# Two groups' expert choice in five pieces, their places and scatters three steps later

## The chip, the cores and the metric

The kernel runs on one core of a Trainium2 chip, as one launch. The metric is the device time of that launch in microseconds (us), lower is better. The core's engines work in parallel, each through its own instruction queue in order: TensorE (PE, with its weight loads PEld), VectorE (DVE), ScalarE (ACT), GpSimd (POOL), and the DMA queues, of which SyncE (SP) and ScalarE issue plain transfers and GpSimd the indirect ones. They synchronise by semaphores.

## The reference

Two layers over x of shape 32 x 128 x 128 (batch row, token, feature), float32. Layer 0 is cross attention with 16 heads of width 8 and a mixture of 8 experts; layer 1 is cross attention with 16 heads of width 64 and a quantised feed-forward net. The change touches the routing of layer 0:

```python
x = x + xattn0(layernorm(x), ctx, ctx)
# routing, on inputs = layernorm(x):
num = einsum('bsd,ed->bse', inputs, waff)
aff = num / (norm(inputs) * norm(waff) + 1e-09)
tcr = one_hot(argmax(softmax(aff)), 8)            # each token's one expert
ecr = (rank of the token in its row by aff) < cap
out = sum over experts e of gelu(xi @ W1[e] + b1[e]) @ W2[e] + b2[e],  xi = inputs * (tcr * ecr)[e]
x = x + out
```

The kernel sorts the tokens by expert before the expert stage: each token gets a place (a row of the buffer sorted_x), and an indirect DMA scatters a batch row's 128 tokens there.

## The kernel before

**Stages.** Layer 0's attention with the routing woven in (0 to about 245 us of the span), the experts (to about 348 us), layer 1 (to the end). The change lies in the first stage.

**Steps.** The first stage is a loop over 32 batch rows, b = 0 to 31, written once for each engine; the same b on all engines is called a step. TensorE's step b: scores(b) (L366), minus_max(b, 0) (L373), route_transpose(b-4) (L307), places(q) in some steps (L341 to L346), back_transposes(b-1) (L392), minus_max(b, 1), affinity(b-4) (L325), max_scores(b+1, 0) (L357), o_transpose(b-1) (L397), x_transpose(b+2), minus_max(b, 2 and 3), output(b-1) (L401), projections(b+2) (L312 to L314), max_scores(b+1, 1), values(b) (L385).

VectorE's step b: locate(q) in some steps, normalise(b-1) (L595, L598; it waits for the back transposes), num_copy(b-4) (L542), x_stats(b+4), two maxima (L589), residual(b-1) (L604), choose(q) in some steps, q_spread(b+2) (L531; it waits for the projections), v_copy(b+2) (L537), two maxima, residual_stats(b-1) (L608, L610).

GpSimd's step b: x_plus(b) (L196, read by residual(b)), route_norm(b-2) (L221 to L225; it waits for residual_stats(b-2) and makes xn2, which route_transpose reads), x_norm(b+4) (L185 to L190; up to step 27), denominators(q) in some steps (L234 to L244), then scatters (L251). ScalarE makes the exponentials and copies, among them route_copy (L465), which takes the routing transpose out of PSUM into r_xnT.

**Groups.** Routing works on groups of batch rows: (0, 8), (8, 16), (16, 24), (24, 28), (28, 32), q = 0 to 4. For a group ending at row z the denominators are made in step z+1, choose(q) in step z+3 (ten small VectorE instructions, L550 to L569, each waiting for the one before by the semaphore choice), places(q) on TensorE and locate(q) on VectorE (four instructions, L576 to L583) in step z+4. That is steps 11 and 12 for group 0, 19 and 20 for group 1, 27 and 28 for group 2; groups 3 and 4 lie at the loop's end and behind it.

**Waits.** route_transpose(r) waits until v_copy(r+5) is done, since it writes the PSUM bank that the projections were read from. places(q) waits for tcrb of its group and for the route_copy of the routing transpose just ahead of it. The affinity after it waits for the first instruction of locate(q), which reads the places from the same bank. A scatter waits for all four of locate(q). At the loop's start ScalarE's DMA queue clears sorted_x, in steps 1 to 12.

**Scatters.** From step 13 on, GpSimd issues one scatter a step where a located row is left (group 0: steps 13 to 20, group 1: steps 21 to 28), and up to three a step from step 29; the rest follow behind the loop. Only when all 32 have landed does the expert stage load its first tile.

Of the kernel before, what the change touches and what calls it, by code (L numbers as in the profile page):

```python
# [5 lines left out]
ALU = mybir.AluOpType  # L6
# [65 lines left out]
def attention_routing_block(nc, ctx, space, consts, x, ctxT, w, wr, x_res, xn2, stats2, psum, dram):  # L72
# [7 lines left out]
    E = 8  # L80
    GROUPS = ((0, 8), (8, 16), (16, 24), (24, 28), (28, 32))
    NG = len(GROUPS)
    group_at = {z - 1: q for q, (a, z) in enumerate(GROUPS)}
    group_of = {r: q for q, (a, z) in enumerate(GROUPS) for r in range(a, z)}
    SCALE = float(HD) ** -0.5
    LOADS = ((0, 1), (1, 2), (2, 4), (4, 8), (8, 16), (16, 32))
# [91 lines left out]
    def pool_part(g, after_setup, before_last):  # L178
# [84 lines left out]
        for b in range(B):  # L263
            if b == 1:
                expert_norms()
            x_plus(b, b % 2)
            if b >= 2:
                route_norm(b - 2)
            if b + 4 < B:
                x_norm(b + 4, b % 2)  # L270
            if b - 2 in group_at:
                denominators(group_at[b - 2])
            located = max([z for a, z in GROUPS if z + 5 <= b], default=0)
            for _ in range(1 if b < 29 else 3):
                if b >= 13 and scattered < located:
                    scatter(scattered)
                    scattered += 1
        route_norm(B - 2)
# [9 lines left out]
    def tensor_part(pe):  # L288
# [31 lines left out]

        def affinity(r):
            pe.wait_ge(rsem["xnT"], r + 1)
            if r - 1 in group_at:
                pe.wait_ge(rsem["place"], 4 * group_at[r - 1] + 1)
            nc.tensor.matmul(nump, rt["xnT"][:, r % 2, :], rt["waffT"][:], start=True, stop=True).then_inc(rsem["num_done"], 1)  # L325

        def places(q):
            a, z = GROUPS[q]
            n = z - a
            at_, rows = placep[:, 0:n * E], rt["tcrb"]  # L330
            pe.wait_ge(rsem["choice"], 10 * q + 7)
            pe.wait_ge(rsem["set"], 7)
            if z + 5 <= B:
                pe.wait_ge(rsem["xnT"], z + 1)
            else:
                pe.wait_ge(rsem["num"], z)
            wait(pe, rsem["choice"], 10 * (q - 1) + 10)
            if q == NG - 1:
                pe.wait_ge(rsem["choice"], 10 * q + 10)
                nc.tensor.matmul(countp, rt["ones_b"][:], rt["seen"][:, q + 1, :], start=True, stop=True)  # L340
            nc.tensor.matmul(at_, rt["before_t"][:], rows[:, a:z, :].rearrange("p b e -> p (b e)"),  # L341
                             start=True, stop=False, skip_group_check=True)
            for j in range(n - 1):
                nc.tensor.matmul(placep[:, E * (j + 1):E * n], rt["ones_b"][:], rows[:, a + j:a + j + 1, :].broadcast_to([P, n - 1 - j, E]),
                                 start=False, stop=False, skip_group_check=True)
            nc.tensor.matmul(at_, rt["ones_b"][:], rt["seen"][:, q:q + 1, :].broadcast_to([P, n, E]),  # L346
                             start=False, stop=True, skip_group_check=True).then_inc(rsem["place_done"], 1)
# [60 lines left out]
        for b in range(B):  # L408
            s, more = b % 2, b + 2 < B
            scores(b)  # L410
            minus_max(b, 0)
            if b >= 4:
                route_transpose(b - 4)
            if b - 5 in group_at:
                places(group_at[b - 5])
            if b == 0:
                expert_sums()
            else:
                back_transposes(b - 1, 1 - s)
            minus_max(b, 1)  # L420
            if b >= 4:
                affinity(b - 4)
            if b + 1 < B:
                max_scores(b + 1, 0)
            if b >= 1:
                o_transpose(b - 1, 1 - s)
            if more:
                x_transpose(b + 2, s)
            minus_max(b, 2)
            minus_max(b, 3)  # L430
            if b >= 1:
                output(b - 1, 1 - s)
            if more:
                projections(b + 2, s)
            if b + 1 < B:
                max_scores(b + 1, 1)
            values(b)
# [77 lines left out]
    def vector_part(dve):  # L515
# [25 lines left out]
            dve.wait_ge(rsem["num_done"], r + 1)  # L541
            nc.vector.tensor_copy(rt["num"][:, r, :], nump).then_inc(rsem["num"], 1)  # L542

        def choose(q):
            a, z = GROUPS[q]
            cols, n, seq, first = slice(a, z), z - a, rsem["choice"], 10 * q
            aff, tcr, shape = rt["aff"][:, cols, :], rt["tcr"][:, cols, :], [P, z - a, E]
            tmp, score, smax = rt["tmp"][:, 0:n, :], rt["score"][:, 0:n, :], rt["smax"][:, 0:n]
            dve.wait_ge(rsem["den"], 5 * q + 5)
            nc.vector.reciprocal(tmp, rt["den"][:, q % 2, 0:n, :]).then_inc(seq, 1)  # L550
            dve.wait_ge(seq, first + 1)
            dve.wait_ge(rsem["num"], z)
            nc.vector.tensor_tensor(aff, rt["num"][:, cols, :], tmp, ALU.mult).then_inc(seq, 1)
            dve.wait_ge(seq, first + 2)
            nc.vector.tensor_reduce(rt["mval"][:, cols], aff, AX_X, ALU.max).then_inc(seq, 1)
            dve.wait_ge(seq, first + 3)
            nc.vector.tensor_tensor(tmp, aff, rt["mval"][:, cols].unsqueeze(2).broadcast_to(shape), ALU.is_equal).then_inc(seq, 1)
            dve.wait_ge(seq, first + 4)
            dve.wait_ge(rsem["set"], 6)
            nc.vector.tensor_tensor(score, tmp, rt["weight"][:].unsqueeze(1).broadcast_to(shape), ALU.mult).then_inc(seq, 1)  # L560
            dve.wait_ge(seq, first + 5)
            nc.vector.tensor_reduce(smax, score, AX_X, ALU.max).then_inc(seq, 1)
            dve.wait_ge(seq, first + 6)
            nc.vector.tensor_tensor(rt["tcrb"][:, cols, :], score, smax.unsqueeze(2).broadcast_to(shape), ALU.is_equal).then_inc(seq, 1)
            nc.vector.tensor_tensor(tcr, score, smax.unsqueeze(2).broadcast_to(shape), ALU.is_equal).then_inc(seq, 1)
            dve.wait_ge(seq, first + 8)
            nc.vector.tensor_reduce(rt["gsum"][:], tcr.rearrange("p b e -> p e b"), AX_X, ALU.add).then_inc(seq, 1)
            dve.wait_ge(seq, first + 9)
            nc.vector.tensor_tensor(rt["seen"][:, q + 1, :], rt["seen"][:, q, :], rt["gsum"][:], ALU.add).then_inc(seq, 1)  # L569

        def locate(q):
            a, z = GROUPS[q]
            cols, n, seq, first = slice(a, z), z - a, rsem["place"], 4 * q
            place = rt["place"][:, 0:n, :]
            dve.wait_ge(rsem["place_done"], q + 1)
            nc.vector.tensor_tensor(place, placep[:, 0:n * E].rearrange("p (b e) -> p b e", e=E),  # L576
                                    rt["region"][:].unsqueeze(1).broadcast_to([P, n, E]), ALU.add).then_inc(seq, 1)
            dve.wait_ge(seq, first + 1)
            nc.vector.tensor_tensor(place, place, rt["tcr"][:, cols, :], ALU.mult).then_inc(seq, 1)
            dve.wait_ge(seq, first + 2)  # L580
            nc.vector.tensor_reduce(rt["posf"][:, cols], place, AX_X, ALU.add).then_inc(seq, 1)
            dve.wait_ge(seq, first + 3)
            nc.vector.tensor_copy(rt["pos_s"][:, cols], rt["posf"][:, cols]).then_inc(seq, 1)  # L583

        def maxima(b, s, k):
            dve.wait_ge(max_done, 4 * b + k + 1)
# [33 lines left out]
            maxima(0, 0, k)  # L620
        for b in range(B):
            s, more = b % 2, b + 2 < B
            if b - 5 in group_at:
                locate(group_at[b - 5])
            if b == 0:
                dve.wait_ge(rsem["wsum_done"], 1)
                nc.vector.tensor_copy(rt["wsum"][:], yp[:, 0:E]).then_inc(rsem["wsum"], 1)
            else:
                normalise(b - 1, 1 - s)
            if b >= 4:  # L630
                num_copy(b - 4)
            if b + 4 < B:
                x_stats(b + 4, s)
            if b + 1 < B:
                maxima(b + 1, 1 - s, 0)
                maxima(b + 1, 1 - s, 1)
            if b >= 1:
                residual(b - 1, 1 - s)
            if b - 4 in group_at:
                choose(group_at[b - 4])  # L640
            if more:
                q_spread(b + 2, s)
                v_copy(b + 2, s)
            if b + 1 < B:
                maxima(b + 1, 1 - s, 2)
                maxima(b + 1, 1 - s, 3)
            if b >= 1:
                residual_stats(b - 1, 1 - s)
# [1579 lines left out]
```

## Time and profile before

| | |
|---|---|
| median of 3 runs | 924.01 us (922.65 to 928.94) |
| profiled execution | 923.75 us |
| its span, first to last instruction | 922.0 us |
| mean granted TensorE clock | 0.970 of full |
| busy share of the span: PE, DVE, ACT, POOL | 92%, 74%, 47%, 52% |

The page gives the span in 40 slices of 23 us with each engine's busy share; the first stage fills the first eleven. A timeline row gives start, duration, engine, line, operation, output and inputs, the count merged into the row, and in brackets the idle time ahead of it with what ended that.

### The profile page before, as it was taken

The page shows a single profiled execution, that of the slowest core. Times are in us where ns is not written, and L with a number is a line of the kernel's source. Part 1 is how long each engine was busy: PE and PEld are TensorE (multiplying, and loading weights), DVE is VectorE, ACT ScalarE, POOL GpSimd, SP SyncE. Part 2 cuts the span into 40 slices and gives each one's busy share as a digit, 9 for nine tenths or more (in the row PEclk, how much of TensorE's full clock was granted, in tenths as well). Part 3 has the DMA queues.
Part 4 walks back from the last instruction along what each step waited for, and adds up shares of the span by engine and source line. Part 5 has one row for each costly group of instructions (what it writes and reads, how often), then busy time and mean ns, then how long its engine had stood idle before and what let it go on. Part 6 is the DMA issues. An engine that isn't in the chain of part 4 may idle for free.

```text
span 922.0 us, 28047 instructions
## 1 busy us (share of the span) xinstructions
PE 849.0 (92%) x9989; PEld 682.0 (74%) x10019; DVE 683.1 (74%) x1915; ACT 432.4 (47%) x1010; POOL 482.7 (52%) x977
## 2 busy tenths in 40 slices
PE   2999999997599997999999999999999999999964
PEld 1677777765598885787877878878878788787752
DVE  2688888886524565588888888888888888888866
ACT  1566565654156563335354454444544545444432
POOL 5567687877522224245554654545646555454331
PEclk9999999999799997999999999999999999999995
DMA  7666430001556650121121121211212112112120
GB/s 206 224 247 242 157 102 15 14 14 33 154 141 169 160 154 26 34 57 33 33 63 37 45 54 34 62 37 34 62 36 54 45 34 62 37 34 57 28 56 9
DMA packets 57980, 71.33 MB, mean 77 GB/s; under 512 B 8051, under 2 KB 34547, under 8 KB 57843
## 3 DMA queue, kind: packets, MB, share of 16 engines
q1 hardware_dynamic: 43842, 45.48, 19.2%
q10 hardware_dynamic: 11952, 19.86, 5.8%
q0 software_dynamic: 2048, 4.20, 1.5%
q8 instruction: 82, 1.34, 0.6%
q14 instruction: 56, 0.45, 0.2%
HBM read 45.13 MB, written 24.38 MB: 75 GB/s over the span
## 4 chain that ended last, share of the span: by engine, by line
PE 81%; DVE 7%; POOL 5%; issue 4%; DMA 1%; ACT 1%; SPq 1%; DVEq 0%; POOLq 0%; ACTq 0%
PE psum L1596 8%; PE psum L1526 7%; PE psum L1613 7%; PE psum L1517 7%; PE psum L1575 6%; PE psum L1555 6%; PE psum L868 4%; PE psum L1601 4%; PE psum L1624 3%; PE psum L858 3%; PE psum L366 3%; PE psum L373 2%; PE psum L1586 2%; PE psum L385 2%; PE psum L357 1%
## 5 line engine op out<-in xcount | busy, mean ns | idle before, releaser
L1768 ACT ACTIVATE a_pT<-psum 128x512 f32<-128x512 f32 x128 | 69.5, 595 | 53.9 <-PE psum L1601 53.9
L1360 POOL TENSOR_TENSOR f_hd<-f_hmc,f_wmean 128x1 f32<-128x1 f32 x32 | 6.8, 211 | 151.6 <-DVE f_hr L2020 151.6
L1526 PEld LDWEIGHTS psum<-a_cTm,a_Wk 128*128 128x128 f32 x512 | 62.9, 194 | 28.6 <-issue 27.2
L589 DVE TENSOR_REDUCE l_mx<-psum 128x4 bf16<-128x512 f32 x128 | 81.5, 678 | 1.8 <-PE psum L357 1.4
L1907 DVE TENSOR_REDUCE a_mxf<-psum 128x4 f32<-128x512 f32 x128 | 80.9, 672 | 1.3 <-PE psum L1586 1.3
L1596 PE MATMUL psum<-a_qT,a_kT 64*128 64x128 f32 x1024 | 74.4, 285 | 5.2 <-ACT a_v L1790 1.1
L1517 PEld LDWEIGHTS psum<-a_xT,a_Wq 128*128 128x128 f32 x512 | 66.1, 196 | 15.3 <-issue 14.4
L475 ACT ACTIVATE l_pT<-psum 128x512 f32<-128x512 f32 x128 | 70.5, 597 | 11.7 <-PE psum L373 11.5
L1526 PE MATMUL psum<-a_cTm,a_Wk 128*128 128x128 f32 x512 | 74.0, 289 | 1.9 <-POOL a_cTm L1317 1.1
L1596 PEld LDWEIGHTS psum<-a_qT,a_kT 64*128 64x128 f32 x1024 | 62.1, 187 | 14.5 <-issue 14.0
L1517 PE MATMUL psum<-a_xT,a_Wq 128*128 128x128 f32 x512 | 71.1, 283 | 0.5 <-ACT a_xT L1751 0.5
L1575 PE MATMUL psum<-a_Wv,a_cTm 128*128 128x512 f32 x128 | 69.9, 628 | 1.2 <-DVE a_kT L1895 0.7
L1613 PE MATMUL psum<-a_pT,a_v 128*64 128x128 f32 x1024 | 70.0, 279 | 0.0
L1895 DVE TENSOR_TENSOR a_kT<-psum,a_nkm 128x512 f32<-128x512 f32 x64 | 42.5, 664 | 36.5 <-PE psum L1526 36.5
L1555 PE MATMUL psum<-a_Wo,a_oT 128*128 128x128 f32 x512 | 64.3, 280 | 5.5 <-DVE a_oT L1930 5.5
L1555 PEld LDWEIGHTS psum<-a_Wo,a_oT 128*128 128x128 f32 x512 | 61.4, 196 | 6.1 <-DVE a_oT L1930 6.0
L1808 ACT COPY f_hqT<-psum 128x512 bf16<-128x512 bf16 x32 | 18.7, 585 | 99.9 <-PE psum L1661 99.9
L827 POOL COPY e_w2t<-e_w 128x512 f32 x39 | 24.3, 625 | 74.5 <-PE psum L868 74.5
L1613 PEld LDWEIGHTS psum<-a_pT,a_v 128*64 128x64 f32 x1024 | 54.6, 136 | 11.2 <-issue 7.0
L1354 POOL TENSOR_SCALAR f_hq<-f_ht 128x512 bf16<-128x512 f32 x29 | 56.5, 1948 | 2.3
L373 PEld LDWEIGHTS psum<-negI,l_mx 128*128 128x128 bf16 x512 | 36.4, 103 | 25.9 <-DVE l_mx L589 22.7
L1790 ACT COPY a_v<-psum 128x512 f32<-128x512 f32 x64 | 37.5, 585 | 25.4 <-PE psum L1575 25.4
(298 smaller groups left out, 2180.9 us busy)
## 6 DMA issues: line engine op xcount, KB each, us to landing
sorted_x<-r_zeros ACTq DMA_DIRECT2D x12, 1408.0 KB, 5.9
a_r_all<-a_r_rows SPq DMA_DIRECT2D x64, 256.0 KB, 4.0
e_w<-in_E_W1b SPq DMA_DIRECT2D x39, 258.0 KB, 2.8
e_xt<-sorted_x SPq DMA_DIRECT2D x39, 64.0 KB, 2.4
sorted_y<-e_yt ACTq DMA_DIRECT2D x39, 64.0 KB, 2.4
a_cin<-in_ctx SPq DMA_DIRECT2D x32, 64.0 KB, 3.7
out<-f_x SPq DMA_DIRECT2D x32, 64.0 KB, 3.2
x_res<-in_x SPq DMA_DIRECT2D x1, 512.0 KB, 5.9
```

Source lines behind the costliest of these rows:

```text
L373: last = nc.tensor.matmul(tp[k][:, j * S:(j + 1) * S], mx[:, b % 2, h:h + 1].to_broadcast([P, P]), negI[:], start=False, stop=(j == Q4 - 1 ...
L475: nc.scalar.activation(pT[:, k, :], tp[k], ACT.Exp, scale=SCALE).then_inc(exp_ready, 1)
L589: nc.vector.tensor_reduce(mx[:, s, Q4 * k:Q4 * k + Q4], maxp[k % 2].rearrange("p (h t) -> p h t", h=Q4), AX_X, ALU.max).then_inc(mx_ready, 1)
L1354: nc.gpsimd.tensor_scalar(hq[:], ht[:], -M, 127.0, ALU.add, ALU.min).then_inc(hq_ready, 1)
L1517: last = nc.tensor.matmul(bank[:, i * S:(i + 1) * S], Wq[:, 4 * half + i, :], xT[:, b % 2, :], start=True, stop=True)
L1526: last = nc.tensor.matmul(bank[:, i * S:(i + 1) * S], Wk[:, 4 * half + i, :], cTm[:, b % 2, :], start=True, stop=True)
L1555: nc.tensor.matmul(pa[:, 0:D], oT[:, p, :], Wo[:, p, :], start=(p == 0), stop=False)
L1575: nc.tensor.matmul(bank, cTm[:, b % 2, :], Wv[:, 512 * half:512 * half + 512], start=True, stop=True).then_inc(v_done, 1)
L1596: nc.tensor.matmul(tp[e][:, i * S:(i + 1) * S], kT[r, b % 2, p, :], qT[r, b % 2, p, :], start=(i == 0), stop=False, skip_group_check=True)
L1613: last = nc.tensor.matmul(op[half][e * HD:(e + 1) * HD, i * S:(i + 1) * S], v[:, b % 2, 8 * half + 4 * e + i, :], pT[:, 2 * half + e, i * ...
L1768: nc.scalar.activation(pT[:, 2 * half + e, :], tp[e], ACT.Exp, scale=SCALE).then_inc(exp_ready, 1)
L1907: nc.vector.tensor_reduce(mxf[:, hh:hh + 4], maxp[e].rearrange("p (h t) -> p h t", h=Q4), AX_X, ALU.max).then_inc(mxf_ready, 1)
```

## The change

choose(q) is cut into five functions. For groups 0 and 1 (SPREAD = 2) one of them runs in each of the steps z+2 to z+6 (10 to 14, 18 to 22), at the place in the step where choose stood. places(q) and the first half of locate(q) move from step z+4 to z+7 (15 and 23), and locate's second half to the place of the choice pieces in the same step. The affinity's wait moves with them; places(q) waits for the route_copy of its new step. Scatters start the step after: group 0 in steps 16 to 23, one a step; group 1 in steps 24 to 27, two a step. Groups 2 to 4 stay as they were. No instruction's operands change.

```diff
+    SPREAD = 2
+    close_at = {z + (7 if q < SPREAD else 4): q for q, (a, z) in enumerate(GROUPS)}
...
-            located = max([z for a, z in GROUPS if z + 5 <= b], default=0)
-            for _ in range(1 if b < 29 else 3):
-                if b >= 13 and scattered < located:
+            located = max([GROUPS[q][1] for c, q in close_at.items() if c < b], default=0)
+            for _ in range(1 if b < 24 else 2 if b < 29 else 3):
+                if scattered < located:
                     scatter(scattered)
...
         def affinity(r):
             pe.wait_ge(rsem["xnT"], r + 1)
-            if r - 1 in group_at:
-                pe.wait_ge(rsem["place"], 4 * group_at[r - 1] + 1)
+            if r + 4 in close_at:
+                pe.wait_ge(rsem["place"], 4 * close_at[r + 4] + 1)
...
         def places(q):
-            if z + 5 <= B:
+            if q < SPREAD:
+                pe.wait_ge(rsem["xnT"], z + 4)
+            elif z + 5 <= B:
                 pe.wait_ge(rsem["xnT"], z + 1)
...
-            if b - 5 in group_at:
-                places(group_at[b - 5])
+            if b in close_at:
+                places(close_at[b])
...
+        def choose_spread(q, part):      # 0 reciprocal, 1 affinity, 2 score, 3 expert, 4 seen
...
-            if b - 5 in group_at:
-                locate(group_at[b - 5])
+            if b in close_at:
+                locate_rows(close_at[b])
+                if close_at[b] >= SPREAD:
+                    locate_position(close_at[b])
...
-            if b - 4 in group_at:
+            if b - 4 in group_at and group_at[b - 4] >= SPREAD:
                 choose(group_at[b - 4])
+            for q in range(SPREAD):
+                choose_spread(q, b - GROUPS[q][1] - 2)
+            if b in close_at and close_at[b] < SPREAD:
+                locate_position(close_at[b])
```

## Rows read from the trace of the kernel before

**Rows 1.** Windows: bounds, length, each engine's busy us (instructions), PEclk, DMA share, GB/s.
```profile
96.11:104.53 8.42, 6.63 (x103) 4.84 (x99) 7.50 (x26) 3.81 (x9) 3.63 (x7) 1.00 0.44 172
104.53:110.41 5.88, 5.88 (x94) 4.49 (x90) 4.91 (x15) 3.70 (x9) 3.44 (x7) 1.00 0.64 245
145.68:155.42 9.74, 7.96 (x102) 6.13 (x99) 7.49 (x26) 3.88 (x9) 8.09 (x14) 0.82 0.05 15
196.57:206.51 9.94, 7.99 (x102) 6.13 (x98) 7.22 (x24) 3.88 (x9) 6.46 (x11) 0.83 0.05 16
```

**Rows 2.** Timeline of VectorE, step 10, the query spread of an ordinary step.
```profile
89.36 0.75 DVE L531 SCALAR_TENSOR_TENSOR l_qz<-psum,l_bq,group_rows 128x512 f32<-128x512 f32 x1 [0.58 <-PE psum L314]
```

**Rows 3.** Timeline of VectorE, step 11, group 0's choice and the query spread behind it.
```profile
94.57 0.54 DVE L550 RECIPROCAL r_tmp<-r_den 128x64 f32<-128x64 f32 x1
95.15 0.22 DVE L553 TENSOR_TENSOR r_aff<-r_num,r_tmp 128x64 f32<-128x64 f32 x1
...
95.66 0.41 DVE L557 TENSOR_TENSOR r_tmp<-r_aff,r_mval 128x64 f32<-128x64 f32 x1
...
96.36 0.22 DVE L562 TENSOR_REDUCE r_smax<-r_score 128x8 f32<-128x64 f32 x1
...
96.76 0.22 DVE L565 TENSOR_TENSOR r_tcr<-r_score,r_smax 128x64 f32<-128x64 f32 x1
...
97.42 0.75 DVE L531 SCALAR_TENSOR_TENSOR l_qz<-psum,l_bq,group_rows 128x512 f32<-128x512 f32 x1
```

**Rows 4.** Timeline of TensorE, step 12, and one row of step 20 (150.82).
```profile
97.19 0.40 PE L373 MATMUL psum<-negI,l_mx 128*128 128x128 bf16 x4
98.51 0.30 PE L307 MATMUL psum<-ident,xy 128*128 128x128 f32 x1 [0.93 <-DVE l_v L537]
99.26 0.19 PE L341 MATMUL psum<-r_tcrb,r_before_t 128*128 128x64 bf16 x1 [0.45 <-ACT r_xnT L465]
...
99.49 0.63 PE L392 MATMUL psum<-ident,l_oev 128*128 128x128 f32 x4
...
101.34 0.33 PE L397 MATMUL psum<-ident,l_on 128*128 128x128 f32 x1 [0.41 <-DVE l_on L598]
...
150.82 0.47 PE L397 MATMUL psum<-ident,l_on 128*128 128x128 f32 x1 [0.37 <-DVE l_on L598]
```

**Rows 5.** Timeline of TensorE, step 18, an ordinary one.
```profile
134.99 0.40 PE L373 MATMUL psum<-negI,l_mx 128*128 128x128 bf16 x4
135.23 0.28 PE L307 MATMUL psum<-ident,xy 128*128 128x128 f32 x1
135.34 0.60 PE L392 MATMUL psum<-ident,l_oev 128*128 128x128 f32 x4
...
136.62 0.33 PE L397 MATMUL psum<-ident,l_on 128*128 128x128 f32 x1
```

**Rows 6.** Timeline of GpSimd, steps 17 to 19, and VectorE's residual of step 19.
```profile
129.90 0.23 POOL L221 TENSOR_SCALAR r_vpe<-stats 128x1 f32<-128x1 f32 x1 [0.54 <-DVE stats L610]
...
138.19 0.46 POOL L196 TENSOR_TENSOR l_xb<-x_res,l_bo 128x128 f32<-128x128 f32 x1
138.74 0.23 POOL L221 TENSOR_SCALAR r_vpe<-stats 128x1 f32<-128x1 f32 x1
...
144.03 0.24 POOL L221 TENSOR_SCALAR r_vpe<-stats 128x1 f32<-128x1 f32 x1
...
144.03 0.28 DVE L604 TENSOR_TENSOR x_res<-psum,l_xb 128x128 f32<-128x128 f32 x1
```

**Rows 7.** Timeline of GpSimd, start of step 29, and two scatters of step 30.
```profile
204.44 0.45 POOL L196 TENSOR_TENSOR l_xb<-x_res,l_bo 128x128 f32<-128x128 f32 x1 [0.77 <-DVE x_res L604]
208.38 0.23 POOL L221 TENSOR_SCALAR r_vpe<-stats 128x1 f32<-128x1 f32 x1 [3.49 <-DVE stats L610]
...
219.25 1.08 POOL L251 DMA_INDIRECT sorted_x<-xy,r_pos_s  x1 [0.18 <-POOL xy L225]
220.63 0.96 POOL L251 DMA_INDIRECT sorted_x<-xy,r_pos_s  x1 [0.30 <-issue]
```

More of the change, by code:

```diff
@@ L542, in num_copy, with choose_reciprocal, choose_affinity @@
             nc.vector.tensor_copy(rt["num"][:, r, :], nump).then_inc(rsem["num"], 1)
-        def choose(q):
+        def choose_reciprocal(q):
+            a, z = GROUPS[q]
+            n, seq = z - a, rsem["choice"]
+            dve.wait_ge(rsem["den"], 5 * q + 5)
+            nc.vector.reciprocal(rt["tmp"][:, 0:n, :], rt["den"][:, q % 2, 0:n, :]).then_inc(seq, 1)
+        def choose_affinity(q):
             a, z = GROUPS[q]
             cols, n, seq, first = slice(a, z), z - a, rsem["choice"], 10 * q
[L547 to L550, printed above, removed]
+            aff, tmp = rt["aff"][:, cols, :], rt["tmp"][:, 0:n, :]
             dve.wait_ge(seq, first + 1)
@@ L555, in choose, with choose_score @@
             nc.vector.tensor_reduce(rt["mval"][:, cols], aff, AX_X, ALU.max).then_inc(seq, 1)
+        def choose_score(q):
+            a, z = GROUPS[q]
+            cols, n, seq, first = slice(a, z), z - a, rsem["choice"], 10 * q
+            aff, tmp, score, shape = rt["aff"][:, cols, :], rt["tmp"][:, 0:n, :], rt["score"][:, 0:n, :], [P, z - a, E]
             dve.wait_ge(seq, first + 3)
@@ L560, in choose, with choose_expert @@
             nc.vector.tensor_tensor(score, tmp, rt["weight"][:].unsqueeze(1).broadcast_to(shape), ALU.mult).then_inc(seq, 1)
+        def choose_expert(q):
+            a, z = GROUPS[q]
+            cols, n, seq, first = slice(a, z), z - a, rsem["choice"], 10 * q
+            score, smax, shape = rt["score"][:, 0:n, :], rt["smax"][:, 0:n], [P, z - a, E]
             dve.wait_ge(seq, first + 5)
@@ L564, in choose, with choose_seen @@
             nc.vector.tensor_tensor(rt["tcrb"][:, cols, :], score, smax.unsqueeze(2).broadcast_to(shape), ALU.is_equal).then_inc(seq, 1)
+        def choose_seen(q):
+            a, z = GROUPS[q]
+            cols, n, seq, first = slice(a, z), z - a, rsem["choice"], 10 * q
+            score, smax, tcr, shape = rt["score"][:, 0:n, :], rt["smax"][:, 0:n], rt["tcr"][:, cols, :], [P, z - a, E]
             nc.vector.tensor_tensor(tcr, score, smax.unsqueeze(2).broadcast_to(shape), ALU.is_equal).then_inc(seq, 1)
@@ L569, in choose, with locate_rows @@
             nc.vector.tensor_tensor(rt["seen"][:, q + 1, :], rt["seen"][:, q, :], rt["gsum"][:], ALU.add).then_inc(seq, 1)
-        def locate(q):
+        def choose(q):
+            choose_reciprocal(q)
+            choose_affinity(q)
+            choose_score(q)
+            choose_expert(q)
+            choose_seen(q)
+        def choose_spread(q, part):
+            if part == 0:
+                choose_reciprocal(q)
+            elif part == 1:
+                choose_affinity(q)
+            elif part == 2:
+                choose_score(q)
+            elif part == 3:
+                choose_expert(q)
+            elif part == 4:
+                choose_seen(q)
+        def locate_rows(q):
             a, z = GROUPS[q]
@@ L579, in locate, with locate_position @@
             nc.vector.tensor_tensor(place, place, rt["tcr"][:, cols, :], ALU.mult).then_inc(seq, 1)
+        def locate_position(q):
+            a, z = GROUPS[q]
+            cols, n, seq, first = slice(a, z), z - a, rsem["place"], 4 * q
             dve.wait_ge(seq, first + 2)
-            nc.vector.tensor_reduce(rt["posf"][:, cols], place, AX_X, ALU.add).then_inc(seq, 1)
+            nc.vector.tensor_reduce(rt["posf"][:, cols], rt["place"][:, 0:n, :], AX_X, ALU.add).then_inc(seq, 1)
             dve.wait_ge(seq, first + 3)
             nc.vector.tensor_copy(rt["pos_s"][:, cols], rt["posf"][:, cols]).then_inc(seq, 1)
+        def locate(q):
+            locate_rows(q)
+            locate_position(q)
         def maxima(b, s, k):
```

## Prediction

> **What bounds the kernel now.** The change touches the first stage only, 32 steps of attention with the routing to experts woven in, so I read that stage. First, the table of windows, one window to a step of TensorE's program [rows 1]. An ordinary step takes 5.88 us, TensorE is busy for all of it, VectorE for 4.91 and GpSimd for 3.44: TensorE sets the pace, VectorE has about 1 us to spare. Three steps are longer: step 12 with 8.42 us, step 20 with 9.74, step 28 with 9.94; TensorE's busy time stays below the step's length in each. Against 5.88 they cost 2.54, 3.86 and 4.06 us. The last is group 2's, which the change leaves alone. So 6.40 us is all that the two reorganised groups cost the loop.
>
> Second, VectorE's timeline. In an ordinary step it idles 0.58 us ahead of the query spread (L531), waiting for the projections [rows 2]. In step 11 ten small instructions of the expert choice stand in that place, from 94.57 to 97.42: 2.85 us [rows 3].
>
> Third, TensorE's timeline of step 12 against ordinary step 18 [rows 4, 5], taken as start to start distances:
> - L373 to L307 is 1.32 us instead of 0.24: 1.08 too long, idle on l_v. The routing transpose waits for the value copy, queued on VectorE behind the choice.
> - L307 to L392 is 0.98 instead of 0.11: 0.87 for the places, most of it a wait for ScalarE's copy r_xnT.
> - L392 to L397 is 1.85 instead of 1.28: 0.57, idle on l_on. VectorE is still late, and its four place instructions stand ahead of the normalisation.
>
> That makes 2.52 of the 2.54. Step 20 has the same three parts and one more: from L397 to the next step's start TensorE takes 4.60 us (150.82 to 155.42), where step 12 takes 3.19 (101.34 to 104.53) for the same matmuls. The granted clock was 1.00 in step 12 and 0.82 over step 20 [rows 1, 4]: there it fell from the upper to the lower of its two levels, 2.4 to 1.2 GHz, after idle pieces much like those of step 12, and that took 1.41 us.
>
> Last, GpSimd. Its routing, denominators and scatters set the tail: from 208.38, when it starts L221 after waiting 3.49 us for VectorE's statistics, its queue runs almost without a gap to the end of the stage [rows 7]. What VectorE and TensorE gain before that point therefore reaches the end, unless GpSimd itself gets there late.
>
> **The change, part by part.** *The choice in five pieces.* The same ten instructions run. From their starts [rows 3] the pieces take 0.58 us (reciprocal), 0.51 (affinity, maximum), 0.70 (two products), 0.40 (maximum, tcrb), and 0.66 (tcr, sum, seen). They go into steps 10 to 14 and 18 to 22, just ahead of the query spread where 0.58 us is idle [rows 2]. The largest overshoot is 0.12. Nobody waits for that: the whole choice made VectorE 2.85 - 0.58 = 2.27 late and TensorE lost 1.08, so the value copy has 1.19 us in hand. Cost 0. If that idle time were gone, each piece would delay the spread by its full length, still below 1.19. The first piece needs the denominators one step sooner: for group 1 it follows the residual of step 18, one step of 5.88 us ahead of the one at 144.03, so at 138.15. GpSimd starts x_plus at 138.19 [rows 6], and a scatter of over 1 us lies between the denominators and that: they are about 1 us early.
>
> *The places three steps later.* Nine small matmuls, the routing transpose before them and the wait for r_xnT are the same in steps 15 and 23: 0.87 each stays. VectorE is now on time. Its first two place instructions run while TensorE does the four back transposes that the normalisation waits for, so the 0.57 goes. The last two stand ahead of the query spread, at 0.40 us by the like pair L562 and L564 in rows 3, again under the idle 0.58. The affinity's wait for the first place instruction moves along with the places, with the same back transposes in between: cost 0.
>
> *Stalls saved.* Two times (1.08 + 0.57) = 3.30, and 1.41 for the clock that fell in step 20: 4.71. The other way round, 6.40 less two times 0.87 is 4.66. I take 4.66. TensorE idles about half a microsecond in one piece where it idled in three, and the full stall of step 12 did not lower the clock, so I expect no fall.
>
> *The scatters.* Group 0's go out in steps 16 to 23, group 1's two a step in steps 24 to 27, none in step 28. A scatter starts 1.38 us after the one ahead of it [rows 7]. GpSimd's step with one scatter, without waits, is 5.29 us (138.74 to 144.03), and one with denominators 8.84, which leaves it 2.96 behind the 5.88 of the loop [rows 6]. With a second scatter a step takes 6.67. Lateness after step 24: 0.79; after step 25, with group 2's denominators: 4.54; then 5.33, and 6.12 at the start of step 28. Before it was 2.96 - 2 x 0.59 = 1.78 there. The 4.34 more shrink to 2.96 since step 28 has no scatter, and GpSimd idles 0.77 + 3.49 = 4.26 there [rows 7]. Margin: 1.30 us. Does anybody want its work sooner? x_plus, 2.96 late at 138.65, is read by the residual at 144.03 [rows 6]: 5.38 left, 8.3 in all, against 5.33 at step 27. Cost 0, with 3 us in hand.
>
> The Trainium skill (SBUF — State Buffer, "SBUF: two separate sides") says that VectorE with two SBUF inputs and GpSimd lock a shared pair of ports against each other for a whole instruction. It speaks against small two-input pieces beside more scatters. The trace has something like it: L557 and L560 together took 0.70 us, L562 and L564 of the same size 0.40 [rows 3]. By the rule such tenths go from either engine's margin, and the sum stays.
>
> *Sum.* The profiled execution took 923.75 us, a span of 922.0 and 1.75 around it. 923.75 - 4.66 = 919.1. The median of the runs is 924.01, 0.26 above it: **919.3 us**, 0.5% less. Bounds of the saving: above 6.40, if nothing were left of the two stalls, and 1.41 more if step 28 kept its clock; below 3.25, if the clock fall of step 20 should count for nothing, since the stall would on average not have had it.
>
> **Rivals.**
> - *The clock takes part back.* Steps 15 and 23 still have an idle piece. Against: step 12's three pieces left the clock up. For: steps 20 and 28 are hardly worse and lost it. One fall costs 1.41 (920.7), two 2.82 (922.1). The Trainium skill (TensorE: Matmul & The Clock Gate, "What's actually happening") has the activity judged in windows that run freely, not tied to the program; then equal stalls may fare differently, as steps 12 and 20 did.
> - *It falls better.* Everything behind step 12 moves by some us. If the stall of step 28 keeps the upper clock, another 1.41 go, less what GpSimd's margin of 1.30 cuts: about 918.0; with a like fall in a later stage gone too, 916.6.
> - *GpSimd enters the tail late: slower.* Place: L221 of step 29. Price: the four second scatters, each 1.38 by the row, plus any contention. Beyond the margin each us goes straight to the end. It eats the saving when they cost (1.30 + 4.66) / 4 = 1.49 us more each, 2.87 in all. At 3.3 us each: 7.7 - 1.3 - 4.66 = 1.7 over before, 925.7. For: GpSimd runs with no gap for four steps, which before it never did. Against: in step 30 three scatters follow each other, the second of them after 1.38 [rows 7].
> - *No gain.* The spread pieces stretch every one of ten steps by their 0.5 us, because TensorE's program in truth hangs on VectorE: 10 x 0.57 = 5.7 takes all back, 924.9. Against: VectorE idles 0.58 at that point in ordinary steps and TensorE never waits.
>
> **How the numbers follow.** Forecast 0.60 (own range 918.2 to 920.5). Clock takes part back 0.18. Falls better 0.12. GpSimd late 0.05. No gain 0.05. The time is the likeliest one's, 919.3. The range takes in the clock's three cases and leaves out the two last ones: 916.5 to 922.8. A measurement of this kernel tells about 1% from no change, 9.2 us, more than the whole 6.40 at stake: faster by over 1% 0.03, slower by over 1% 0.02, within 0.95.
>
> **What would show it.** Right: steps 12 and 20 take 5.88 to 6.0 us; steps 15 and 23 about 6.75, with one idle piece on r_xnT and none on l_v or l_on; no gap over 0.2 us between a choice piece and L531; GpSimd without idle time from step 24 to 28 and a short wait before step 29's L221; this L221 at about 203.7. Wrong: steps 10 to 14 over 6 us, granted clock under 1 in steps 15 or 23, an L221 of step 29 that follows at once on x_plus, or any TensorE or VectorE wait on l_xb, xy or l_xn in steps 26 to 29.

## The result and the profile after

| | before | changed |
|---|---|---|
| median | 923.28 us (20 runs) | 919.89 us (20 runs) |
| ratio to before | | 0.9961, 95% interval 0.9946 to 0.9975 |
| a second set of runs of both | 924.37 (23) | 919.64 (12), ratio 0.9947, 0.9927 to 0.9968 |
| profiled execution's span | 922.0 | 916.1 |

The change gains 0.4 to 0.5%, 3.6 to 4.9 us by the two ratios, where 4.66 was forecast; the measured median lies 0.6 us over the forecast 919.3. One of the changed kernel's 20 runs took 2012.23 us, more than twice the others; the ratio leaves it out, and the median would be 919.86 without it. Lines from 86 on stand a little lower in the changed file: L370 is the old L366 (scores), L377 the old L373, L309 the old L307, L345 the old L341, L396 the old L392, L401 the old L397, L535 the old L531, L659 the old L610, L223 the old L221. The kernels of the experiments shift by some lines again; there the operation and its tiles tell which it is.

First the windows, one to a step: steps 12, 15, 20, 23 and 28 of the changed kernel, and step 28 of a second execution of it (bounds, length, busy us of each engine, granted clock, DMA share, GB/s).

```profile
93.18:99.06 5.88, 5.88 (x94) 4.49 (x90) 5.27 (x17) 3.70 (x9) 3.63 (x7) 1.00 0.65 248
110.81:117.78 6.97, 6.38 (x102) 4.77 (x98) 5.84 (x18) 3.81 (x9) 3.63 (x7) 1.00 0.00 1
141.30:147.18 5.88, 5.88 (x93) 4.49 (x89) 5.28 (x17) 3.70 (x9) 5.19 (x11) 1.00 0.04 14
158.94:165.81 6.87, 6.31 (x102) 4.76 (x98) 5.67 (x19) 3.81 (x9) 5.68 (x10) 1.00 0.04 13
189.33:200.42 11.09, 9.33 (x102) 7.29 (x99) 7.99 (x25) 3.88 (x9) 9.15 (x15) 0.69 0.08 26
```

```profile
191.71:201.96 10.25, 8.08 (x102) 6.13 (x99) 7.67 (x25) 3.88 (x9) 9.03 (x15) 0.83 0.09 28
```

Against [rows 1]: steps 12 and 20 are ordinary now, 5.88 instead of 8.42 and 9.74. Steps 15 and 23 carry the places, 1.09 and 0.99 us over 5.88. The loop gains 6.40 - 2.08 = 4.32 us there. Step 28, which was not edited, got longer: 11.09 instead of 9.94, at a granted clock of 0.69 instead of 0.83; in the second execution 10.25, at 0.83.

TensorE in step 15, with [rows 4, 5] as the rows of before:

```profile
112.12 0.28 PE L309 MATMUL psum<-ident,xy 128*128 128x128 f32 x1
112.85 0.19 PE L345 MATMUL psum<-r_tcrb,r_before_t 128*128 128x64 bf16 x1 [0.45 <-ACT r_xnT L469]
...
113.09 0.63 PE L396 MATMUL psum<-ident,l_oev 128*128 128x128 f32 x4
...
114.39 0.33 PE L401 MATMUL psum<-ident,l_on 128*128 128x128 f32 x1
...
115.91 0.39 PE L316 MATMUL psum<-l_wv,l_cT 128*128 128x128 f32 x2
116.44 0.40 PE L361 MATMUL psum<-l_kT,l_qz 32*128 32x128 bf16 x8
```

The wait for r_xnT is there as before, L309 to L396 takes 0.97 us against the ordinary 0.11, and nothing waits for l_v or l_on. The other 0.21 us of this step lie between L316 and L361, 0.53 us instead of 0.32. L361's weight load waits there for VectorE's maxima (L638), and these started late:

```profile
116.44 0.23 PEld L361 LDWEIGHTS psum<-l_kT,l_qz 32*128 32x128 bf16 x8 [0.33 <-DVE l_mx L638]
```

```profile
115.09 1.29 DVE L638 TENSOR_REDUCE l_mx<-psum 128x4 bf16<-128x512 f32 x2 [0.27 <-issue]
```

"issue" says that the 0.27 us ahead of L638 waited for nothing that the profile shows. All eight profiles of a kernel that puts its places in step 15 have this idle piece, and step 9 has one of 0.26 us in all twelve, before included. So it is no chance and does not come of the places as such; why VectorE paused there stays open.

VectorE in step 13, a piece of two instructions, and the group that stayed whole, in step 27 (only its first row, the two that got longer and the spread behind it):

```profile
103.49 0.21 DVE L579 TENSOR_REDUCE r_smax<-r_score 128x8 f32<-128x64 f32 x1
103.73 0.23 DVE L581 TENSOR_TENSOR r_tcrb<-r_score,r_smax 128x64 bf16<-128x64 f32 x1
104.15 0.75 DVE L535 SCALAR_TENSOR_TENSOR l_qz<-psum,l_bq,group_rows 128x512 f32<-128x512 f32 x1 [0.19 <-ACT l_kT L474]
...
187.88 0.54 DVE L552 RECIPROCAL r_tmp<-r_den 128x64 f32<-128x64 f32 x1
...
189.41 0.29 DVE L572 TENSOR_TENSOR r_score<-r_tmp,r_weight 128x64 f32<-128x64 f32 x1 [0.21 <-DVE r_tmp L569]
...
189.99 0.33 DVE L581 TENSOR_TENSOR r_tcrb<-r_score,r_smax 128x64 bf16<-128x64 f32 x1
...
190.91 0.75 DVE L535 SCALAR_TENSOR_TENSOR l_qz<-psum,l_bq,group_rows 128x512 f32<-128x512 f32 x1
```

The piece lies in the idle time ahead of the query spread, 0.19 us of which is left. In the steps 10 to 14 and 18 to 22 the spread starts 5.09 to 5.12 us behind the step's start (104.15 - 99.06 in step 13), as in step 10 of before (5.09), so no piece delayed it. In step 27 the whole choice takes 3.03 us (187.88 to 190.91), where before it took 2.84 (195.12 to 197.96). Two instructions with both inputs in SBUF grew, to 0.29 and 0.33 us, where before they took 0.23 and 0.22 in the same step. TensorE's wait behind it, in step 28 of before and of the changed kernel:

```profile
199.05 0.30 PE L307 MATMUL psum<-ident,xy 128*128 128x128 f32 x1 [1.01 <-DVE l_v L537]
```

```profile
192.01 0.30 PE L309 MATMUL psum<-ident,xy 128*128 128x128 f32 x1 [1.20 <-DVE l_v L541]
```

GpSimd from the end of step 27 to step 29:

```profile
188.06 1.08 POOL L253 DMA_INDIRECT sorted_x<-xy,r_pos_s  x1 [0.18 <-issue]
189.44 0.96 POOL L253 DMA_INDIRECT sorted_x<-xy,r_pos_s  x1 [0.30 <-issue]
...
197.02 0.47 POOL L198 TENSOR_TENSOR l_xb<-x_res,l_bo 128x128 f32<-128x128 f32 x1
...
199.24 0.45 POOL L198 TENSOR_TENSOR l_xb<-x_res,l_bo 128x128 f32<-128x128 f32 x1
201.99 0.24 POOL L223 TENSOR_SCALAR r_vpe<-stats 128x1 f32<-128x1 f32 x1 [2.30 <-DVE stats L659]
```

Two scatters, the second 1.38 us behind the first, as in [rows 7], and both run beside the whole choice above. Ahead of step 29's L223 GpSimd has 2.30 us of idle time left; [rows 7] had 0.77 + 3.49.

The span fell by 5.9 us, more than the change explains. A part is chance at the start: step 1 begins at 28.81 in this execution, at 31.66 in that of before, and between 29.6 and 32.2 in the ten others. Times below are therefore also given from the start of step 1 to TensorE's first work on a sorted tile (the transpose of e_xt, at 244.11 in the changed kernel's first profile), "the routed stretch": 218.94 and 219.12 us in two executions of before, 215.30 and 214.82 in two of the changed kernel. That is 4.0 us less. It is gained ahead of the tail: step 29's L223 comes 173.18 and 172.43 us behind the start of step 1, against 176.72 and 176.78 for the old L221, 3.9 less on average, and from there to the last L223 both kernels take 23.70 to 23.73 us.

### The profile page after: what moved, and what is told of

Read it like the earlier page. It is cut to its first block, busy times and chain, and to the rows that moved or that the text cites. A ratio compares the mean times of both kernels' runs of the same rounds, so it can differ in the third digit from the quotient of the medians.

```text
span 916.1 us, 28047 instructions
## 1 busy us (share of the span) xinstructions
PE 847.1 (92%) x9989; PEld 680.3 (74%) x10019; DVE 683.1 (75%) x1915; ACT 432.1 (47%) x1010; POOL 481.7 (53%) x977
## 4 chain that ended last, share of the span: by engine, by line
PE 87%; DVE 5%; issue 3%; POOL 2%; DMA 1%; ACT 1%; SPq 1%; DVEq 0%; POOLq 0%; ACTq 0%
PE psum L1651 8%; PE psum L1581 8%; PE psum L1668 7%; PE psum L1572 7%; PE psum L1630 6%; PE psum L1610 6%; PE psum L923 4%; PE psum L1656 4%; PE psum L370 4%; PE psum L1679 3%; PE psum L913 3%; PE psum L389 3%; PE psum L377 3%; PE psum L1641 2%; PE psum L361 2%
## 5 line engine op out<-in xcount | busy, mean ns | idle before, releaser
L638 DVE TENSOR_REDUCE l_mx<-psum 128x4 bf16<-128x512 f32 x128 | 81.7, 680 | 2.2 <-PE psum L361 1.5
L377 PEld LDWEIGHTS psum<-negI,l_mx 128*128 128x128 bf16 x512 | 35.9, 102 | 25.9 <-DVE l_mx L638 24.3
```

The source lines that it names most:

```text
L377: last = nc.tensor.matmul(tp[k][:, j * S:(j + 1) * S], mx[:, b % 2, h:h + 1].to_broadcast([P, P]), negI[:], start=False, stop=(j == Q4 - 1 ...
L638: nc.vector.tensor_reduce(mx[:, s, Q4 * k:Q4 * k + Q4], maxp[k % 2].rearrange("p (h t) -> p h t", h=Q4), AX_X, ALU.max).then_inc(mx_ready, 1)
```

## The experiments

### The choice whole, the places late

```diff
-            if b - 4 in group_at and group_at[b - 4] >= SPREAD:
+            if b - 4 in group_at:
                 choose(group_at[b - 4])
-            for q in range(SPREAD):
-                choose_spread(q, b - GROUPS[q][1] - 2)
```

> The changed kernel with the choice of groups 0 and 1 whole again (2.85 us in steps 11 and 19), its places and scatters still three steps later. My account (the l_v stall is the choice's alone, the l_on stall is that of the four place instructions behind a late VectorE): step 12 takes 5.88 + 1.08 = about 7.0 us with an idle piece on l_v and none on l_on; steps 15 and 23 stay at 6.9 to 7.0; per group 1.1 us more than the changed kernel, 2.2 us in all, so ratio to before about 0.9985 against 0.996. Rival (the gain comes from moving the places, the size of the pieces hardly matters): steps 12 and 20 stay near 5.88. Rival (the l_on stall also belongs to the choice): steps 12 and 20 take 5.88 + 1.65 = 7.5.

Ratio 0.9991 (0.9969 to 1.0013), median 924.10: no change against before that the runs can tell. TensorE, step 12:

```profile
97.48 0.40 PE L377 MATMUL psum<-negI,l_mx 128*128 128x128 bf16 x4
98.90 0.30 PE L309 MATMUL psum<-ident,xy 128*128 128x128 f32 x1 [1.02 <-DVE l_v L541]
99.04 0.60 PE L396 MATMUL psum<-ident,l_oev 128*128 128x128 f32 x4
...
100.89 0.33 PE L401 MATMUL psum<-ident,l_on 128*128 128x128 f32 x1 [0.39 <-DVE l_on L647]
```

Windows of steps 12, 15 and 20:

```profile
96.41:104.07 7.66, 6.19 (x94) 4.56 (x90) 6.80 (x23) 3.70 (x9) 3.23 (x7) 1.00 0.50 191
115.83:122.79 6.96, 6.37 (x103) 4.76 (x99) 5.84 (x18) 3.81 (x9) 3.62 (x7) 1.00 0.00 1
147.01:156.05 9.04, 7.73 (x93) 5.89 (x89) 6.97 (x23) 3.81 (x9) 7.37 (x12) 0.81 0.03 9
```

Moving the places alone brings nothing: both stalls stay. L396 to L401 is 1.85 us, 0.57 too long as in [rows 4], though no place instruction of VectorE is near. So the stall on l_on belongs to the choice as well, not to the four place instructions; my first account had that wrong and the second rival, 7.5, is close to the 7.66. Step 20 has the same two stalls and lost the upper clock on top (0.81). The routed stretch is 221.15 us, 2 more than before: steps 12 and 20 are 0.76 and 0.70 us shorter, but steps 15 and 23 pay 1.08 and 0.98 for the places, step 28 took 11.31, and step 18 took 6.58 with a pause of TensorE for which the trace shows no wait.

### How large a piece may be

```diff
-                choose_spread(q, b - GROUPS[q][1] - 2)
+                for part in {3: (0, 1, 2), 4: (3, 4)}.get(b - GROUPS[q][1], ()):
+                    choose_spread(q, part)
```

> Two pieces instead of five: the first three (1.79 us) in steps 11 and 19, the last two (1.06) in steps 12 and 20. The allowance ahead of the query spread is 0.58 idle + 1.19 in hand = 1.77. My account: steps 11, 12, 19, 20 and 21 all take 5.88 to 5.95, no idle piece of TensorE on l_v. Rival (any piece over the 0.58 idle costs its overshoot): 1.2 us for the first piece and 0.5 for the second in each group, steps of 7.1 and 6.4.

The second kernel has `{3: (0, 1, 2, 3), 4: (4,)}` there. Each of the two was run once (921.40 and 921.88 us), so only their traces are read.

> The first four pieces together (2.19 us by the changed kernel's starts) in steps 11 and 19, the fifth alone a step later. My account: 2.19 - 1.77 = 0.4 us too long, so TensorE idles about 0.2 to 0.4 us on l_v in steps 12 and 20, which take 6.1 to 6.3. Rival (threshold at the idle 0.58): 1.6 us, steps of 7.5.

Their step 12, the first kernel's (97.35 on), then the second's:

```profile
97.35 0.40 PE L377 MATMUL psum<-negI,l_mx 128*128 128x128 bf16 x4
97.60 0.30 PE L309 MATMUL psum<-ident,xy 128*128 128x128 f32 x1
97.74 0.60 PE L396 MATMUL psum<-ident,l_oev 128*128 128x128 f32 x4
...
99.59 0.33 PE L401 MATMUL psum<-ident,l_on 128*128 128x128 f32 x1 [0.39 <-DVE l_on L647]
```

```profile
95.84 0.40 PE L377 MATMUL psum<-negI,l_mx 128*128 128x128 bf16 x4
96.59 0.30 PE L309 MATMUL psum<-ident,xy 128*128 128x128 f32 x1 [0.36 <-DVE l_v L541]
96.73 0.60 PE L396 MATMUL psum<-ident,l_oev 128*128 128x128 f32 x4
...
98.58 0.33 PE L401 MATMUL psum<-ident,l_on 128*128 128x128 f32 x1 [0.39 <-DVE l_on L647]
```

With 1.79 us nothing waits for l_v, as expected; but L396 to L401 is 1.85 again, 0.57 too long, and steps 12 and 20 take 6.49 and 6.43, not the expected 5.88 to 5.95. With 2.19 the l_v stall of step 12 is 0.75 - 0.24 = 0.51 (0.4 was expected), the l_on stall the same 0.57, and steps 12 and 20 take 7.00 and 6.87 (6.1 to 6.3 was expected). So there are two reserves behind the 0.58 of idle time. The value copy's is 2.19 - 0.58 - 0.51 = 1.10 us, near the 1.19 that I had. The normalisation's is smaller: 1.79 - 0.58 - 0.57 = 0.64. That makes about 1.2 us for a piece with no cost at all, by the count. By this trace both are smaller: the first piece took 1.68 us up to the spread, not 1.79, and the spread of step 11 started 6.11 us behind the step's start instead of 5.09, 1.02 late. So the normalisation has 1.02 - 0.57 = 0.45 us in hand, and a measured piece of 1.68 - 0.57 = 1.11 us is free. For the value copy the second kernel gives 1.52 late less 0.51 lost, 1.01. Two reserves would also explain why the l_on stall does not exceed 0.57 in these kernels: a later VectorE stops TensorE at l_v first, and both then move together. Neither rival holds, since the threshold is not at 0.58. The routed stretches are 216.81 and 218.03 us.

### Does GpSimd set the tail?

```diff
+            if b == 28:
+                for k in range(3):
+                    nc.gpsimd.tensor_tensor(rt["pad"][:, k, :], half[:, 0:8], half[:, 0:8], ALU.pow)
```

> The changed kernel with three more instructions on GpSimd in step 28, each like L236 (1.68 us, some 1.76 start to start), 5.3 us in all; their results are used by nothing. My account (GpSimd sets everything from step 29's L221 on; the margin ahead of it is 1.2 to 1.3 us when step 28 takes 9.94, 2.3 when it takes 11.1): no wait ahead of step 29's L221, the expert stage's first tile 3.0 to 4.1 us later relative to step 28's end, the kernel 3 to 4 us slower than the changed one, ratio to before about 1.000. Rival (the tail waits for something else, TensorE or the DMA, and GpSimd has slack to the end): under 1 us, ratio 0.996.

```profile
200.09 4.88 POOL L275 TENSOR_TENSOR r_pad<-half 128x8 f32<-128x8 f32 x3
204.93 0.46 POOL L198 TENSOR_TENSOR l_xb<-x_res,l_bo 128x128 f32<-128x128 f32 x1
205.35 0.24 POOL L223 TENSOR_SCALAR r_vpe<-stats 128x1 f32<-128x1 f32 x1
```

The three instructions took 4.84 us from the first to the start of L198. Step 29 starts at 201.36, so L223 comes 3.99 us behind it instead of 1.57: 2.42 later, the rest went into the idle 2.3. The routed stretch is 218.92 us, 3.6 to 4.1 longer than the changed kernel's. Of that, 0.8 to 1.1 us lie between the tail's last L223 and the first expert tile (19.50 us there against 18.41 and 18.66 in the changed kernel's two executions), so what L223 itself handed on is some 2.5 to 3.3 us: it comes 175.72 us behind the start of step 1, against 173.18 and 172.43. From it to the last L223 this kernel takes 23.70 us, as the changed one does (23.71 and 23.73), so none of its lateness is made up on the way. The ratio, 0.9976 (0.9956 to 0.9996), has the whole kernel 1.4 us slower than the changed one by its first set of runs and 2.7 by its second, with intervals that overlap. That GpSimd's L223 passes its lateness on is shown by the trace; its size in the whole time is not better known than 0 to 4 us.

### Group 2 as well

The changed kernel with these tables, and the same conditions written with them:

```diff
-    SPREAD = 2
+    SPREAD = 3
+    PIECES = {0: {2: (0,), 3: (1,), 4: (2,), 5: (3,), 6: (4,)}, 1: {2: (0,), 3: (1,), 4: (2,), 5: (3,), 6: (4,)},
+              2: {2: (0,), 3: (1, 2), 4: (3, 4)}}
+    CLOSE = (7, 7, 5, 4, 4)
...
-            for _ in range(1 if b < 24 else 2 if b < 29 else 3):
+            for _ in range(1 if b < 24 else 2 if b < 29 else 4):
```

> The changed kernel with group 2's choice also in pieces (0.58 us in step 26, 1.21 in step 27, 1.06 in step 28), its places in step 29 instead of 28, no scatters in step 29 and four each in steps 30 and 31. My account (a piece up to about 1.17 us, the 1.79 less the 0.61 that it cost, is free; from step 29 on GpSimd sets everything): step 28 takes 5.9 instead of 11.1, step 29 about 6.9, TensorE idle on l_v nowhere; GpSimd has no wait left ahead of step 29's L223, which gains its former wait of 2.2 us and no more, so 2.2 us faster than the changed kernel though the loop itself gains 4; ratio to before about 0.994. Rival (TensorE sets the stage's end): 4 us or more faster, ratio 0.992. Rival (the expert stage's start hangs on the transfers of the last scatters): no gain.

Ratio 0.9919 (0.9889 to 0.9948), median 917.93. Steps 28 and 29, and GpSimd's L226 (the old L221) of steps 29 and 30:

```profile
191.65:197.53 5.88, 5.88 (x94) 4.49 (x90) 5.63 (x18) 3.70 (x9) 5.19 (x9) 1.00 0.08 26
197.53:204.39 6.86, 6.30 (x102) 4.75 (x98) 5.65 (x18) 3.81 (x9) 5.99 (x12) 1.00 0.06 19
```

```profile
201.92 0.22 POOL L226 TENSOR_SCALAR r_vpe<-stats 128x1 f32<-128x1 f32 x1
...
206.78 0.22 POOL L226 TENSOR_SCALAR r_vpe<-stats 128x1 f32<-128x1 f32 x1
```

The trace is as expected: the two doubled pieces (1.21 and 1.06 us by the count, 1.07 and 1.19 in this execution, in steps 27 and 28) cost nothing, step 28 is ordinary, GpSimd comes without a wait, and the routed stretch is 212.91 us, 2.2 less than the mean of the changed kernel's two. Up to the start of step 29 TensorE gained 5.2 and 4.4 us against these two; GpSimd took the difference. The ratio alone does not decide: it lies at the rival's 0.992, and its interval holds the expected 0.994 too. The stretch and the next run do.

The same kernel with `1 if b < 29 else 3 if b < 30 else 4` scatters a step:

> As the run before, but with one scatter a step up to step 28 and three in step 29, so that three more scatters (3.8 us) lie behind step 29's L223. My account (GpSimd's total work sets the end): L223 of step 29 is about 4.9 us earlier than in the changed kernel, the tail behind it 3.8 longer, 0.7 to 1.1 us faster than the changed one in all, ratio about 0.995. Rival (TensorE sets it): as fast as the run before, with 4 us.

Ratio 0.9946 (0.9922 to 0.9970), median 919.86, routed stretch 214.79 us: 0.3 less than the changed kernel's mean, a little under what was expected. TensorE's loop is as short as in the run before, and step 29's L226 comes 2.01 us behind the step's start instead of 4.39, but with three more scatters behind it. From this L226 to the last one GpSimd takes 27.50 us, against 23.50 in the run before with three scatters fewer. TensorE does not set the end of the stage; what GpSimd still has to do behind step 29's L226 does.

### Three pieces, places two steps sooner

```diff
+    PIECES = {q: {2: (0,), 3: (1, 2), 4: (3, 4)} for q in range(3)}
+    CLOSE = (5, 5, 5, 4, 4)
...
+            for _ in range(1 if b < 27 else 2 if b < 29 else 4):
```

> All three groups of eight with the choice in three pieces (0.58, 1.21 and 1.06 us in steps z+2 to z+4) and the places in step z+5, two steps sooner than in the changed kernel. One scatter a step from step 14, two in steps 27 and 28, four in steps 30 and 31. My account (a piece up to about 1.2 us is free, so five pieces and three steps' delay are not needed; the sooner scatters unload GpSimd ahead of the tail): steps 11, 12, 19, 20, 27, 28 take 5.9, steps 13, 21 and 29 about 6.9; L223 of step 29 comes 1.6 to 2.0 us after the step's start instead of 4.4 with group 2 alone reorganised, no scatter of group 1 is left behind it, so about 2.3 us faster than that kernel: ratio to before 0.989 to 0.992. Rival (pieces over the idle 0.58 cost): 0.6 and 0.5 us a group more, no gain over it.

Ratio 0.9927 (0.9900 to 0.9953), median 918.71, over the expected 0.989 to 0.992, though the interval reaches into it; routed stretch 212.82 us, the same as with group 2 above. GpSimd in steps 29 and 30:

```profile
201.38 0.25 POOL L225 TENSOR_SCALAR r_vpe<-stats 128x1 f32<-128x1 f32 x1
...
207.72 0.22 POOL L225 TENSOR_SCALAR r_vpe<-stats 128x1 f32<-128x1 f32 x1 [1.54 <-DVE stats L661]
```

The pieces do cost almost nothing (steps 11, 12, 19, 20 and 27 take 5.88, step 28 6.04; places in step 13 cost 0.87, in step 21 1.23, with 0.19 us of it idle on l_on). But the further 2.3 us did not come. Step 29's L225 did come 1.5 us sooner than in the kernel with group 2 alone (169.30 against 170.79 us behind the start of step 1), and then this was lost. With group 1's scatters gone, GpSimd has too little to do in step 29 and waits 1.54 us for VectorE's statistics in step 30, while group 2's eight scatters can't start sooner. What moved ahead left a hole. Of the two kernels that beat the changed one neither is better than the other.

### The kernels again, and shifted

> The changed kernel again. The steps that it changed cost 1.1 us over the ordinary one in step 15 and 1.0 in step 23, every time, and nothing in steps 12 and 20. The first step's length and the low clock in step 28 vary from one execution to the next. Ratio to before between 0.995 and 0.998.

Steps 15 and 23 took 6.96 and 6.86 us, steps 12 and 20 5.88, step 28 10.25. The ratio is the second set's in the table above, 0.9947, a little under the expected 0.995.

> The kernel before again, for its steps. Steps 12 and 20 are 2.5 us over the ordinary 5.88 where the clock stays up, 3.9 or more where it falls. My account (which of the two it is varies from one execution to the next): at least one of the two differs from the first profile. Rival (it is tied to the place in the program): step 12 with 8.4 and step 20 with 9.7 again.

Steps 12, 20 and 28 took 8.43, 9.79 and 9.99 us (one run, 926.66 us). These are the outcomes of the first profile: my account failed here, and this run alone spoke for the rival.

> The kernel before with one more GpSimd instruction of 1.7 us ahead of the very first normalisation, so that everything behind starts about 1.6 us later. Rival 1 (where the clock falls is a matter of how the stalls lie against something that runs apart from the program): the stalls of steps 12 and 20 change their outcome in about one of two such shifts. Rival 2 (it goes with the step): step 12 keeps the upper clock at 8.4 us, step 20 falls at 9.7 to 9.8, as in both executions of the kernel before.

Steps 12 and 20 of that execution (one run, 923.23 us):

```profile
96.67:106.75 10.08, 8.18 (x103) 6.17 (x99) 7.86 (x28) 3.93 (x9) 3.66 (x7) 0.83 0.40 153
147.91:157.78 9.87, 8.08 (x103) 6.12 (x99) 7.82 (x27) 3.85 (x9) 8.10 (x14) 0.83 0.05 15
```

Step 12, with the same work and nearly the same idle pieces as in [rows 4] (1.03, 0.45 and 0.42 us, against 0.93, 0.45 and 0.41), now lost the upper clock and takes 10.08 us instead of 8.42. So the outcome isn't tied to the step. The 0.1 us more of idle time hardly decides it either: step 20 of before lost the clock with 0.85, 0.56 and 0.37 us, and step 20 of the kernel with the choice whole with two pieces of 0.86 and 0.39, while step 12 of that kernel kept it with 1.02 and 0.39. One shift of one execution does not say how often each comes, and step 20 did not change with it.

## Why the prediction was right, and where it wasn't

- **Pieces in steps 10 to 14 and 18 to 22, cost 0.** Right: steps 12, 13, 14 and 20 take 5.87 to 5.88, and in step 13 0.19 us stays idle ahead of L535. Not even the 0.12 us of overshoot came. The reserve behind it was oversized: I took the value copy's 1.19 for the only one. It is 1.0 to 1.1, and the normalisation's, 0.64 by the count and 0.45 by the trace, binds sooner. The five pieces of at most 0.70 us never came near either.
- **Places stay at 0.87 in steps 15 and 23.** 1.09 and 0.99. In step 23 the wait for r_xnT is the longer of its two sizes (0.56, as in step 20 before). In step 15, 0.21 us came on top, by maxima of VectorE that started late without a named cause. Together 0.34 us of the saving that I counted and did not get.
- **The 0.57 on l_on.** It went, but not for the reason given. It belongs to the choice; the whole choice with late places kept it.
- **4.66 from the loop.** 4.32 came in steps 12 to 23. One sentence failed: "The last is group 2's, which the change leaves alone". Step 28 took 11.09 and 10.25 us against 9.94, 9.99 and 10.03 in two executions of before and the shifted one. Of that, 0.19 us are the stall on l_v, which grew from 1.01 to 1.20 behind a choice of 3.03 us instead of 2.84 (0.19 and 0.20 more, in two executions of each). The rest of the 11.09 goes with the granted clock of 0.69; more on it below. The Trainium skill (SBUF — State Buffer, "SBUF: two separate sides") has a VectorE instruction with two SBUF inputs and a GpSimd one that reads SBUF lock a pair of ports against each other, so that the later one waits. The clearest case is in step 11 of before, in [rows 3]: L557, with two SBUF inputs, starts 0.13 us behind GpSimd's x_plus and ends 0.08 behind it, 0.41 us long. In step 19 it takes 0.23, and the ten instructions 2.67 us instead of the 2.85 that I took for both groups.

```profile
95.53 0.46 POOL L196 TENSOR_TENSOR l_xb<-x_res,l_bo 128x128 f32<-128x128 f32 x1
```

For the scatters the trace agrees only in part. The two that grew in step 27, by 0.06 and 0.11 us, are such instructions beside the second scatter; two more of the kind, beside the first one, kept their 0.22 to 0.23. That the scatters made the choice longer fits all six profiles with doubled scatters beside a whole choice in step 27 (3.03 to 3.10 us, against 2.84 in the three without), but no run changed the scatters alone. That it would hit group 2's choice, on the path, I had not seen.
- **GpSimd's margin.** Forecast 1.30 us with a step 28 of 9.94; measured 2.30 with 11.09 and 1.54 with 10.25, so 1.15 and 1.23 at equal length. The second scatters cost the forecast 1.38. The margin held in both executions and no engine waited for l_xb. Step 29's L223 itself was forecast 4.66 us sooner and came 3.9 sooner on average.
- **The clock.** No fall in steps 15 and 23, in any of eight profiles that have the places there. For the stalls of the kernel before, the fall in step 20 came in both executions, in the shifted one, and in the one with the choice whole; in step 12 in one of these four. Counting the 1.41 us of step 20 in full is thus borne out by these four, but nothing shows that the fall must come, and that step 12 kept its clock was no rule. In step 28 the granted clock was 0.83 in both executions of before and in that of the shifted kernel. With the second scatters in step 27 it was 0.69 or 0.70 in four of six executions and 0.83 in two, the changed kernel having one of each. So this cost of about 1 us can differ from one execution to the next, and it may come more often with the longer stall; the runs don't settle that.
- **The total.** Forecast 919.3, measured 919.9, ratio 0.9949 against 0.9961 with an interval that just holds it; the second set has 0.9947. The routed stretch says 4.0 us. So the mechanism was right in the main and the size some 0.7 us too large; that the median came within 0.6 us is partly luck, as the next figures show. Behind the routed stretch the two kernels do the same, but its time varies a lot by chance: from the first expert tile to the end the executions took 668.2 to 677.5 us. The longest, of the kernel with the choice whole, has a granted clock of 0.61 over 35 us where layer 1 starts (second row); in the changed kernel's first execution the lowest stretch shown there is 25 us at 0.77 (first row):

```profile
345.00:370.00 25.00, 21.59 (x189) 17.04 (x189) 10.53 (x33) 7.98 (x16) 11.35 (x21) 0.77 0.07 19
```

```profile
350.00:385.00 35.00, 28.88 (x199) 22.43 (x198) 13.69 (x41) 9.13 (x17) 13.60 (x29) 0.61 0.06 18
```

## What to carry to other kernels

A block of small instructions in front of a queue's regular work can be free in pieces and dear as a whole; what a piece may cost is the idle time there plus the smallest reserve among all that wait behind it, so follow every reader, not the first one that shows as idle. When the loop is relieved, look who feeds what comes after it: here GpSimd's queue took about half of the next gain, and moving its work forward beyond the point of balance gave nothing more. And compare stretches between two events of the program rather than whole spans where chance outside them is as large as the effect.

## What the runs showed of the hardware that was not expected

- Nearly the same stalls at the same place can keep the upper clock in one execution (step 12, 8.42 and 8.43 us) and lose it in another, of the shifted kernel (10.08), which costs 1.66 us there. With a single idle piece of 0.45 or 0.56 us (steps 15 and 23 of eight profiles) the granted clock stayed 1.00 in all 16 cases.
- The start of the program varies: step 1 began between 28.81 and 32.23 us, the shifted kernel's the latest, with others at 31.9 to 32.1.
- VectorE's small instructions with two inputs in SBUF mostly took 0.22 to 0.23 us. Two of those in step 27 took 0.29 to 0.35 us in the changed kernel's two executions, beside a scatter of GpSimd. L557 took 0.41 in step 11 of before, beside x_plus.
- VectorE pauses about 0.26 us at step 9 in every profile, and at step 15 in those with places there, without a wait that the profile shows.
